# Two attentions: the rows of the maxima of the next batch are sent ahead of both stacks of the batch after it

## The reference

```
layer 0: q = LN(x) Wq, k = ctx Wk, v = ctx Wv;  softmax(q k^T / sqrt(8) + mask) v, then Wo   (512 keys)
layer 2: the same with biases and low-rank terms, att = where(tril(256, 512), att, -inf)     (causal)
x = x + attention(LN(x));  x = x + ffn(LN(x));  ...
```

## Time and profile before

| | us |
|---|---|
| median of 3 runs | 1495.89 (1490.34 to 1503.80) |
| the profiled execution, its own time | 1489.75 |
| its span, first to last instruction | 1488.0 |
| mean granted clock of PE | 0.785 of full speed |

### The profile page before, as it was taken

The page is one execution under the profiler, slowest core; times in us unless marked ns, Lnnn a source line. Parts: engine busy times, 40 slices in busy tenths (PEclk is TensorE's granted clock), DMA queues, the critical chain, the costliest instruction groups (busy, mean ns, idle before and its releaser), DMA issues. The chain is left out here.

```text
span 1488.0 us, 21408 instructions
## 1 busy us (share of the span) xinstructions
PE 965.2 (65%) x6394; PEld 564.5 (38%) x6396; DVE 661.4 (44%) x2199; ACT 487.1 (33%) x975; POOL 443.7 (30%) x690
## 2 busy tenths in 40 slices
PE   4699998779685899367777129992297100799400
PEld 2233333435463565223333116661165000677300
DVE  6588885433334333655663303333355700233222
ACT  2478877412211232244554003330233000233100
POOL 2424320046103004155552340005300177000375
PEclk8599999779857999567885559996598555799755
DMA  5345544000130111233431011111110011355212
GB/s 191 100 140 187 173 144 141 7 0 0 44 130 25 36 42 40 79 100 114 145 117 58 22 46 41 41 41 45 53 36 2 7 51 53 107 143 146 80 53 67
DMA packets 110219, 113.39 MB, mean 76 GB/s; under 512 B 11738, under 2 KB 92396, under 8 KB 108980
## 3 DMA queue, kind: packets, MB, share of 16 engines
q1 hardware_dynamic: 100900, 96.04, 20.8%
q0 software_dynamic: 7168, 14.69, 3.3%
q10 hardware_dynamic: 2064, 1.57, 0.3%
HBM read 66.78 MB, written 45.09 MB: 75 GB/s over the span
## 5 line engine op out<-in xcount | busy, mean ns | idle before, releaser
L1726 POOL DMA_INDIRECT e_back<-rows_out,e_pos x112 | 105.9, 945 | 390.0 <-DMA rows_out<-e_y 356.8
L1717 POOL DMA_INDIRECT rows_in<-xn,e_pos x112 | 109.4, 977 | 257.2 <-DVE e_pos L1879 143.8
L651 DVE TENSOR_REDUCE a_neg_max<-bank 128x1 f32<-128x512 f32 x256 | 163.0, 684 | 44.6 <-PE bank L846 42.6
L711 ACT ACTIVATE wb<-bank 128x512 f32<-128x512 f32 x256 | 145.3, 599 | 48.9 <-PE bank L868 48.4
L1969 PE MATMUL bank<-ident,e_xs 128*128 128x128 f32 x192 | 55.8, 294 | 154.6 <-DMA e_xs<-rows_in 150.4
L2075 DVE COPY e_xT<-bank 128x128 f32<-128x128 f32 (+1 forms) x96 | 40.3, 419 | 174.8 <-PE bank L1969 173.1
L646 DVE CUSTOM_DVE_ANT_0 bank<-bank,a_tri 128x128 f32<-128x128 f32 (+1 forms) x256 | 84.4, 388 | 54.8 <-PE bank L841 54.0
L868 PE MATMUL bank<-a_QS,a_KS 51*128 51x256 bf16 x512 | 94.1, 281 | 15.5 <-DMA a_QS<-a_m_rows 8.4
L846 PE MATMUL bank<-a_KS,a_QS 48*128 48x512 bf16 x256 | 98.7, 419 | 7.0 <-DMA a_QS<-a_q_dram 6.2
L1969 PEld LDWEIGHTS bank<-ident,e_xs 128*128 128x128 f32 x192 | 28.3, 148 | 163.4 <-issue 160.9
L886 PE MATMUL bank<-wb,a_V 128*9 128x256 f32 x1024 | 80.6, 389 | 7.4 <-ACT wb L711 5.8
(11 more groups left out here) (284 smaller groups left out, 2062.2 us busy)
## 6 DMA issues: line engine op xcount, KB each, us to landing
rows_in<-wa SPq DMA_DIRECT2D x8, 1024.0 KB, 9.3
wa<-in_f_w SPq DMA_DIRECT2D x8, 1024.0 KB, 7.3
e_xs<-rows_in SPq DMA_DIRECT2D x32, 256.0 KB, 2.9
rows_out<-e_y SPq DMA_DIRECT2D x32, 256.0 KB, 2.3
a_KS<-a_k_dram SPq DMA_DIRECT2D x32, 192.0 KB
wa<-in_f_w SPq DMA_DIRECT2D x8, 768.0 KB, 7.0
wb<-in_f_w SPq DMA_DIRECT2D x8, 768.0 KB, 10.3
a_QS<-a_q_dram SPq DMA_DIRECT2D x56, 96.0 KB
```

The source lines that it names most:

```text
L651: nc.vector.tensor_reduce(least, a_bank[(2 * n + t) % 3][:, :], AX.X, ALU.max, negate=True).then_inc(max_done, 1)
L711: nc.scalar.activation(E[:, h % EBUFS, 512 * u:512 * u + 512], b_bank[u][:, :], ACT.Exp).then_inc(exp_done, 1)
L1717: pool.indirect_dma_start(out=c.rows_in[:, :], out_offset=bass.IndirectOffsetOnAxis(ap=pos[:, K * t + j:K * t + j + 1], axis=0), in_=c.xn[ ...
L1726: pool.indirect_dma_start(out=back[:, n % BACK, :], out_offset=None, in_=rows_out[:, :], in_offset=bass.IndirectOffsetOnAxis(ap=pos[:, n:n ...
```

## The change

The call of `stack_in(i+2, 0)` moves behind `aug_in(i+1, 0)`. No instruction is added or removed, and no buffer or semaphore is changed.

```diff
@@ -436,10 +436,10 @@
                         load_ctx(i + 3)
                     if i + 2 < B:
                         parts_out(i + 2)
-                        stack_in(i + 2, 0)
                     if i + 1 < B:
                         aug_in(i + 1, 0)
                     if i + 2 < B:
+                        stack_in(i + 2, 0)
                         stack_in(i + 2, 1)
                     background(c, layer, arg, sp, i)
```

## The result

The changed kernel took 1529.93 us (median of 3, 1522.84 to 1530.41) against 1495.89: a ratio of 1.0207, 95% interval 1.0121 to 1.0294. That is 34 us; the forecast was 9 to 12. The profiled execution took 1530.41 us, its span 1528.6.

A forecast was written before the change was run, and what follows sets the result against it. PE was taken to set the pace in layer 0, latency in layer 2. Layer 0's +10.2 us and layer 2's +1.5 made +11.7, on the 1493.1 median 1504.8, forecast 1505; range 1490 to 1519.

The forecast's parts named there:

- The direction and the queue: Slower overall: nothing gained in layer 0, and in both attentions head 8's rows queue behind the background; +11.7 us.
- The delay of the background's end: Layer 0: background ends 2.2 us later (between 1.35 and 2.6), from 1.35 later issue plus stack backlog.
- The slack: Layer 0, pass 0, head 8: rows could come 0.4 us later before PE, ready at 96.68, waited for them.
- I cost that at nothing: Layer 0, head 3 of the next batch: stack half 0 comes later, charged 0 us.
- the term was 10.2: Layer 0, head 8: new PE waits, 1.6 us in passes 0 to 4 and 2.2 in pass 5, +10.2 us.
- rival C: Layer 0: waits of 2 us make PE's clock fall, some 2 us more each of six; +12, 1517; chance 0.14.
- The gain at head 0: Layer 2, six passes with stacks: rows sent ahead of the stack cut PE's waits by at most 8.6 us.
- the term: Layer 2: the wait gained at head 0 comes back at head 8, 6 x 0.25 = +1.5 us.
- The distance from the background's issue to the use of the rows: Layer 2, head 8: taken as 6.7 us, the shorter of two, giving r + 14.5 (r: end of ACT's copy).
- the upper end that I had priced at +9: Layer 2, head 8: with 7.57 us and 0.4 for longer stack backlog, rows come at r + 15.8, +9 us.
- A: Rows pass the background: layer 2 keeps its 8.6 us, layer 0 costs nothing; 1484.5; chance 0.10.
- B: Both halves small: layer 2 gains 3.5 us, layer 0 costs +5.3; +2, 1495; chance 0.18.

The follow-up runs named there:

- e8: Kernel before with one added wait: in layer 0, passes 0 to 5, SP sends the background some 2.2 us later; ratio 1.0013 to the kernel before.
- e1: The change made in layer 0's attention alone, against the kernel before: ratio 1.0154 (23 us slower).
- second pair of profiles: Kernel before and changed kernel each profiled once more with no edit: single executions of 1495.18 and 1531.72 us.
- e2: The change made in layer 2's attention alone, against the kernel before: ratio 1.0056 (8 us slower).
- e3: Changed kernel with each background transfer issued one place later, behind the next pass's rows for head 8: ratio 1.0013 to the kernel before.
- e11: Kernel before with layer 0's background held until ACT is through head 3 of the next batch: ratio 1.0094 to the kernel before.
- e5: Kernel before with SP holding layer 0's rows for head 8 (batches 1 to 7), order of transfers unchanged: ratio 1.0128 to the kernel before.
- e7: Kernel before in layer 0; in layer 2 the change plus the background one place later: 1494.95 us against 1497.68, ratio 0.9993.

## Why the prediction was wrong

**The direction and the queue: right.** Nothing was gained in layer 0, and the rows at head 8 came late behind the background. I gave waits there of 1.8 us in passes 0 to 4; the profile shows 1.73, 1.78, 1.84, 2.47 and 1.61. That the first three fit so well is luck. The delay of the background's end was 2.8 us, not 2.2, and I had its parts in the wrong weight (e8). The slack was about 1 us in pass 0, not 0.4: `rows_in` landed at 95.6 there, 9.2 us after its issue and not the 9.90 of pass 5, and PE was ready at 96.68. And the late half 0, which I had left out, brought PE to head 8 some 0.5 us later. The three errors nearly cancel. Pass 5 was to wait 3 us; it did not, because it had already stood 2.06 us at head 3.

**The step that failed: "I cost that at nothing", of half 0 at head 3.** It is 3.8 us in layer 0. The reason given, that PE would only wait there for what it waits for at head 8 anyway, held in pass 5; in passes 0 to 4 the waits at head 3, 1.7 us in all, come on top. With them the waits for transfers sum to 12.0 us more; the term was 10.2.

**The step that failed most: leaving the clock to rival C.** The forecast charged layer 0 for waiting alone. Its five head-8 waits were each followed by about 3.5 or 7 us at 1.2 GHz, and the wait at head 3 of pass 5 by about 10: together 14.7 us of longer matmuls, more than the waits themselves. C had the mechanism, but a chance of 0.14 and 12 us. I put it aside because "PE is far busier in layer 0". That busyness did not protect the clock: PE was fully busy when it fell (the windows from 97 us on). And the earlier trace rows, 0.98 us of waiting with the clock kept, was a smaller stall than the ones I was forecasting; the row that fitted them was the 2.77 us of the earlier trace rows. With 14.7 added, layer 0 would have stood at 10.2 + 14.7 = 24.9, against the 26.6 of the profiles and the 23 us of e1's launches.

**Layer 2: mis-sized, and less than it looked.** The gain at head 0 came, 9.3 us of waiting. (The prediction's 8.6 for it is a wrong sum: its five waits of 13.4 us less 1.2 each are 7.4.) Head 8 took 4.8 of it back, not all, and head 3, costed at nothing here too, took 6.0. The waits thus came out 1.5 us longer (19.1 against 17.6), the very size of the term, but made up otherwise; PE's waits for the maxima's rows over the whole attention were to stay at 23 to 27 us and fell from 24.7 to 18.5. In the second pair of profiles the waits even fell (12.2 against 14.2). What grew in both pairs is the time of PE's matmuls, by the clock: 16.0 and 7.8 us. The distance from the background's issue to the use of the rows was too short at 6.7 us: in pass 2 it was 744.68 - 736.66 = 8.0 us, r + 15.8, the upper end that I had priced at +9. The term was 1.5 us; e2 measured 8.

**The rivals.** A is out: e3 and e11 show the rows held by the background. B is out: layer 0 cost 23 us, not 5.3, and layer 2 gained nothing. C named what happened in layer 0, and its sign came: over the 285 us of the earlier trace rows the clock was 0.87 where it had been 0.91. What stays open is why the clock falls after some stalls and not after others of the same size (e5), and so how much of layer 2's loss is the order of transfers and how much the place where the clock happens to fall. In layer 0, over all thirteen profiles, PE waited for these transfers 29 times for more than 1.5 us, and in 26 of them the clock fell during the wait or within 1.6 us of its end. The three without a fall (1.58 in e5, 1.96 in e11, 2.07 in e7) are all at head 8 of pass 5. Of the 40 shorter ones that the profiles list, four had a fall, the shortest of them 1.33 us, and the clock never fell there without such a wait.

## What to carry to other kernels

Where one engine issues all transfers in a fixed order to one queue, moving one forward moves others back. Ask for each what it now overlaps and what stands behind it: here a load that nobody was waiting for held up 12 KB that everybody was. Where PE sets the pace, price a new stall of 2 us at about twice its length, since the clock may fall after it (here 12.0 us of waits cost 26.6); check by the granted clock whether any stall that size is already in the trace, and by what followed it. Take two profiles of a stage whose clock wanders before reading a difference of 10 us in it.

## What was not expected of the hardware

- A PE that had run at 2.4 GHz for a whole pass, and was fully busy after the stall, was put to 1.2 GHz from 0.9 us after the end of a 1.73 us wait, for about 7 us. The Trainium skill (TensorE: Matmul & The Clock Gate, HAM oscillation — how this bites in real kernels) describes a like pattern, of DMA waits after which the next tile starts cold. This trace agrees that such waits cost more than their length, with 14.7 us of clock against 12.0 of waits in layer 0; the waits that the page shows are of some 3 to 5 us, and here 1.61 to 2.47 us at head 8 were enough.
- The last 1 MB of the 1.8 MB of background landed some 7.3 us after its issue with no stack near and 11.0 behind a whole stack of 1.15 MB: holding it back 2.2 us (e8) cost layer 0 nothing (158.4 us against 158.6).
- Layer 2's attention, with the same code, took 124.1 to 133.9 us from profile to profile, at clocks from 0.82 down to 0.60.
